# Attention with a top-2 expert layer: constant rows written in place, a looped section for general masks, and expert rows gathered by a row map

## The reference

```python
def _L0_xattn_ref(query, key, value, mask, Wq, bq, Wk, bk, Wv, bv, Wo, bo):
    q = _split_heads(query @ Wq.T + bq)
    k = _split_heads(key @ Wk.T + bk)
    v = _split_heads(value @ Wv.T + bv)
    scores = jnp.einsum('bhqd,bhkd->bhqk', q, k) / jnp.sqrt(jnp.float32(HD))
    scores = jnp.where(mask[:, None, :, :], jnp.finfo(scores.dtype).min, scores)
    attn = jax.nn.softmax(scores, axis=-1)
    ctx = jnp.einsum('bhqk,bhkd->bhqd', attn, v)
    merged = ctx.transpose(0, 2, 1, 3).reshape(query.shape[0], -1, D)
    return merged @ Wo.T + bo

def _L0_ffn_ref(x, gate_w, w1, b1, w2, b2):
    probs = jax.nn.softmax(jnp.einsum('bsd,ed->bse', x, gate_w), axis=-1)
    topk_probs, topk_idx = jax.lax.top_k(probs, TOP_K)
    oh = jax.nn.one_hot(topk_idx, NUM_EXPERTS, dtype=x.dtype)
    h = jnp.einsum('bsd,fed,bske->bskf', x, w1, oh)
    h = jax.nn.gelu(h + jnp.take(b1, topk_idx, axis=0))
    y = jnp.einsum('bskf,def,bske->bskd', h, w2, oh)
    y = y + jnp.take(b2, topk_idx, axis=0)
    return jnp.sum(y * topk_probs[..., None], axis=-2)

x = x + _L0_xattn_ref(_layernorm(x), ctx, ctx, mask, ...)
x = x + _L0_ffn_ref(_layernorm(x), ...)
```

## Time and profile before

| | |
|---|---|
| median of 3 runs | 335.9 us (335.01, 335.9, 337.93) |
| profiled execution | 335.63 us; span 333.9 us; mean granted TensorE clock 0.916 |
| PE busy | 260.5 us (78%) |
| ACT busy | 230.8 us (69%) |
| DVE busy | 170.1 us (51%) |
| POOL busy | 84.7 us (25%) |

### The profile page before, as it was taken

One profiled execution on the slowest core, in us unless ns is written; L12 is line 12 of the kernel. 1 busy time (PEld: TensorE's weight loads), 2 busy tenths in 40 slices (PEclk: granted clock), 3 DMA queues, 4 the chain that ended last, 5 costly groups with the idle time before them and its releaser, 6 DMA issues.

```text
span 333.9 us, 6252 instructions
## 1 busy us (share of the span) xinstructions
PE 260.5 (78%) x1855; PEld 130.2 (39%) x1856; DVE 170.1 (51%) x420; ACT 230.8 (69%) x364; POOL 84.7 (25%) x138
## 2 busy tenths in 40 slices
PE   2587866499999999989899999986484169999940
PEld 2464535122222221212222222235473169999940
DVE  4638966044544535353545454438751047676622
ACT  4366564389999999999999999961794024555520
POOL 8899002100000000000000000402057504444430
PEclk9999895599999999999999999997789559999995
DMA  6999790001101010101001010199201170111115
GB/s 195 381 273 399 291 206 17 5 23 23 34 5 39 0 39 12 28 12 28 18 22 26 14 32 7 39 377 276 36 33 48 48 183 26 32 33 34 31 32 187
DMA packets 29091, 29.57 MB, mean 89 GB/s; under 512 B 15357, under 2 KB 22929, under 8 KB 28944
## 3 DMA queue, kind: packets, MB, share of 16 engines
q1 hardware_dynamic: 27456, 26.21, 26.1%
q0 software_dynamic: 1616, 3.13, 3.2%
HBM read 21.62 MB, written 7.45 MB: 87 GB/s over the span
## 4 chain that ended last, share of the span: by engine, by line
issue 27%; PE 26%; ACT 20%; DVE 7%; DMA 7%; another core or an unknown queue 4%; POOL 3%; SPq 2%; ACTq 1%; DVEq 1%; POOLq 1%
ACT w2T L995 9%; ACT arenaB L995 9%; PE bank L1278 6%; DMA mask_u<-in_mask_BxSxS_bk_dram 5%; PE bank L1397 5%; PE bank L1260 5%; PE bank L1405 3%; DVE arenaB L900 2%; PE bank L1345 2%; PE bank L1169 1%; DMA arenaA<-ys_dram 1%; DVE arenaB L906 1%; PE bank L1355 1%; DVEq L895 1%
## 5 line engine op out<-in xcount | busy, mean ns | idle before, releaser
L717 DVE TENSOR_TENSOR arenaA<-bank,arenaA 128x512 f32<-128x512 f32 x80 | 55.2, 690 | 76.4 <-PE bank L1278 76.4
L995 ACT ACTIVATE arenaB<-bank 128x1024 f32<-128x1024 f32 x80 | 77.5, 1021 | 8.3 <-PE bank L1260 6.2
L995 ACT ACTIVATE w2T<-bank 128x1024 f32<-128x1024 f32 x80 | 76.7, 1030 | 1.3
L1260 PE MATMUL bank<-qS,keys 64*128 64x512 bf16 x324 | 63.2, 389 | 10.1 <-ACT w2T L995 5.7
L1025 ACT ACTIVATE mask_u<-bank,arenaB 128x128 f32<-128x128 f32 x92 | 26.2, 368 | 39.7 <-PE bank L1397 39.7
L1260 PEld LDWEIGHTS bank<-qS,keys 64*128 64x128 bf16 x324 | 15.4, 93 | 97.1 <-ACT w2T L995 49.4
L1278 PE MATMUL bank<-arenaB,vcur 128*32 128x512 f32 x320 | 42.6, 605 | 1.0
L1278 PE MATMUL bank<-w2T,vcur 128*32 128x512 f32 x320 | 42.6, 605 | 0.0
L411 POOL CAST keep<-flags 128x1 f32 x11 | 2.1, 187 | 141.0 <-DVE arenaC L628 140.3
L478 POOL DMA_INDIRECT ys_dram<-arenaB,mask_u x23 | 22.2, 964 | 36.3 <-DVE arenaB L906 36.3
L1397 PE MATMUL bank<-arenaB 128*128 128x128 f32 x184 | 27.4, 296 | 2.8 <-DVE arenaB L892 2.5
(11 more groups left out here) (301 smaller groups left out, 325.7 us busy)
## 6 DMA issues: line engine op xcount, KB each, us to landing
mask_u<-in_L_ffn_w_dram SPq DMA_DIRECT2D x2, 2048.0 KB, 10.6
mask_u<-in_mask_BxSxS_bk_dram SPq DMA_DIRECT2D x6, 560.5 KB, 16.0
ctx_sb<-in_ctx_dram SPq DMA_DIRECT2D x3, 768.0 KB, 13.2
qS<-qparts_dram SPq DMA_DIRECT2D x4, 448.0 KB
mask_u<-in_mask_BxSxS_bk_dram SPq DMA_DIRECT2D x6, 240.0 KB, 11.6
keys_in<-kparts_dram SPq DMA_DIRECT2D x40, 32.0 KB
mask_u<-in_mask_BxSxS_bk_dram SPq DMA_DIRECT2D x1, 1121.0 KB, 8.4
xs_dram<-w1T SPq DMA_DIRECT2D x2, 520.0 KB, 16.8
```

Source lines behind the costliest of these rows:

```text
L717: nc.vector.tensor_tensor(a, bank[:, 4 + k % 2, :], a, ALU.add).then_inc(s["ac"], 1)
L995: nc.scalar.activation(probs[u % 8], bank[:, 2 * (u % 2):2 * (u % 2) + 2, :].rearrange("p a b -> p (a b)"), ACT.Exp, scale=SCALE).then_inc ...
L1260: last = mm(bank[:, 2 * (u % 2) + a, :], keys[rows, g, :], qS[rows, g, cols], start=not hides, stop=True, tile_position=(64 * a, 0))
```

## The change

Ten edits, in the order of the program. Line numbers of the changed kernel are given as "new line".

In the preamble: the constant rows of `qS` come from two memsets on GpSimd instead of a memset and two DMAs. The table `pick` and the third part of the queries are computed on VectorE, between its OR steps, which stand in another order. The first mask tile `mbf` is made on ScalarE. On TensorE the section for `general` masks is a loop over the eight query tiles, with `qcur` copied by GpSimd, instead of written out 16 times; its branch comes after one plan number, and the other two are loaded ahead of the branch on `partial`. The fill of `xs_dram` is gone.

In the second half: rows are no longer scattered with their gates. ScalarE writes all of `xn2` ahead of its weight copies, and SP writes it to `xn_dram` in plain order. VectorE builds 0/1 matrices from the slots, 16 products on TensorE between the two sets of weight transposes turn them into a row map (for each slot the row it holds), and eleven small steps on VectorE, each waiting for the one before, make the row to read and the row to write. GpSimd gathers tiles by indirect DMA, four ahead (`AHEAD`), and in the loop alternates scatter(j) and gather(j+4). Results go to `ys_dram` without gates; the gates come in at the end, with 16 steps of 128 x 128 in place of two adds. The transposes of the gates and the `b2` products moved into the expert loop.

```diff
@@ SP
-            sp.wait_ge(s["scat"], 16 * 2 * QT)
-            for k, (j0, j1) in enumerate(XS_CUTS):
-                sp.dma_start(xs_sb[:, j0:j1, :], xs_dram.rearrange("(j s) c -> s j c", s=P)[:, j0:j1, :]).then_inc(xs_in[k], 16)
+            sp.wait_ge(s["cq_sb"], 2 + QT)
+            sp.dma_start(xn_dram.rearrange("(p t) d -> p t d", t=QT), xn2).then_inc(s["xn_out"], 16)
...
@@ GpSimd, preamble
-            nc.gpsimd.memset(ones_rows, BF16_ONES).then_inc(s["ones_in"], 1)
-            pool.wait_ge(s["ones_in"], 1)
             for w in range(2):
-                pool.dma_start(qS[64 * w:64 * w + 8, :, :].bitcast(F32),
-                               ones_rows.rearrange("p (a q) -> p a q", a=1).broadcast_to([8, G, 512])).then_inc(s["qzero"], 16)
+                nc.gpsimd.memset(qS[64 * w:64 * w + 8, :, :].bitcast(F32), BF16_ONES).then_inc(s["qzero"], 1)
...
-            nc.gpsimd.tensor_scalar(pick, rowkey, iota_p[:, :], None, ALU.is_equal).then_inc(s["pick"], 1)
             pool.wait_ge(s["q_sb"], 2)
             nc.gpsimd.tensor_copy(qparts[:, 1, :], qres).then_inc(s["q_sb"], 1)
-            nc.gpsimd.tensor_tensor(qparts[:, 2, :], qres, qparts[:, 1, :], ALU.subtract).then_inc(s["q_sb"], 1)
...
-            nc.gpsimd.tensor_copy(mbf[:, :, :], mask_u8[:, :, bass.ds(first * P, P)]).then_inc(s["mb"], 1)
...
@@ GpSimd, expert loop
+            def gather(j):
+                nc.gpsimd.indirect_dma_start(xs_sb[:, j, :], None, xn_dram,
+                                             bass.IndirectOffsetOnAxis(ap=x_row[:, j:j + 1].bitcast(U32), axis=0)).then_inc(xs_in[j % AHEAD], 16)
+            pool.wait_ge(s["xn_out"], 16)
+            pool.wait_ge(s["map_sb"], 11)
+            for j in range(AHEAD):
+                gather(j)
             for j in range(NT):
-                pool.wait_ge(s["yacc"], j + 2)
-                nc.gpsimd.indirect_dma_start(ys_dram, bass.IndirectOffsetOnAxis(ap=xs_sb[:, j, ROW - 1:ROW].bitcast(U32), axis=0),
+                pool.wait_ge(s["yacc"], j + 1)
+                nc.gpsimd.indirect_dma_start(ys_dram, bass.IndirectOffsetOnAxis(ap=y_row[:, j:j + 1].bitcast(U32), axis=0),
                                              ysb[:, j % 3, :], None).then_inc(y_out[j % 3], 16)
+                if j + AHEAD < NT:
+                    pool.wait_ge(xs_in[j % AHEAD], 16 * (j // AHEAD + 1))
+                    gather(j + AHEAD)
@@ VectorE, preamble
-            ors(0, 1, 5)
+            ors(0, 1, 2)
+            dve.wait_ge(s["rowkey"], len(COMBOS) + 4)
+            nc.vector.tensor_scalar(pick, rowkey, iota_p[:, :], None, ALU.is_equal).then_inc(s["pick"], 1)
+            ors(0, 2, 4)
...
-            ors(0, 5, QT)
+            ors(0, 4, 6)
+            dve.wait_ge(s["q_sb"], 3)
+            nc.vector.tensor_tensor(qparts[:, 2, :], qres, qparts[:, 1, :], ALU.subtract).then_inc(s["q_sb"], 1)
+            ors(0, 6, QT)
@@ VectorE, behind the slots
+            map_step(nc.vector.tensor_scalar(tile_i, slots, 7, None, ALU.logical_shift_right), 1)
+            map_step(nc.vector.tensor_copy(tile_f, tile_i), 2)
+            map_step(nc.vector.scalar_tensor_tensor(within, tile_f, -float(P), slots_f, ALU.mult, ALU.add), 3)
+            nc.vector.tensor_tensor(in_tile[:, 0:QT, :], cc(within, P)[:, 0:QT, :], iota_q.rearrange("p (a q) -> p a q", a=1).broadcast_to([P, QT, P]), ALU.is_equal)
+            map_step(nc.vector.tensor_tensor(hot_tile, cc(tile_f, NT), ...), 4)
+            nc.vector.tensor_scalar(by_tile[:, :, 0, :], hot_tile, pcol, None, ALU.mult)
+            nc.vector.tensor_tensor(by_tile[:, :, 1, :], hot_tile, cc(ccol, NT), ALU.mult).then_inc(s["map_in"], 1)
+            nc.vector.tensor_tensor(in_tile[:, QT:2 * QT, :], ...).then_inc(s["map_in"], 1)
...
+            dve.wait_ge(s["map_ps"], 1)
+            row_step(nc.vector.tensor_copy(row_f[:, 0:2, 0:NT], bank[:, 2, 0:2 * NT].rearrange("p (a j) -> p a j", a=2)), 1)
+            row_step(nc.vector.tensor_scalar(row_f[:, 2, 0:NT], column, QT - 0.5, None, ALU.is_gt), 2)
...
+            row_step(nc.vector.tensor_copy(y_row, column), 11)
...
-                nc.vector.tensor_scalar(ysb[:, j % 3, :], bank[:, 4 + j % 2, 0:P], xs_sb[:, j, D:D + 1], None, ALU.mult).then_inc(s["yacc"], 1)
+                nc.vector.tensor_copy(ysb[:, j % 3, :], bank[:, 4 + j % 2, 0:P]).then_inc(s["yacc"], 1)
...
-                nc.vector.tensor_tensor(x2, x2, back[k].rearrange("p (t d) -> p t d", d=D), ALU.add).then_inc(s["fin"], 1)
+                for t in range(QT):
+                    nc.vector.scalar_tensor_tensor(x2[:, t, :], back[k][:, t * D:(t + 1) * D], gates[:, k, t:t + 1], x2[:, t, :], ALU.mult, ALU.add).then_inc(s["fin"], 1)
@@ TensorE
-            n = pe.value_load(plan[0:1, 64:65], min_val=1, max_val=T)
             general = pe.value_load(plan[0:1, 65:66], min_val=0, max_val=1)
-            partial = pe.value_load(plan[0:1, 66:67], min_val=0, max_val=T)
             with pe.If(general):
...
+            n = pe.value_load(plan[0:1, 64:65], min_val=1, max_val=T)
+            partial = pe.value_load(plan[0:1, 66:67], min_val=0, max_val=T)
             with pe.If(partial):
...
             expert_weights(0, E)
+            for c in range(2 * QT):
+                last = mm(bank[:, 2, 0:2 * NT], in_tile[:, c, :], by_tile[:, c, :, :].rearrange("p a j -> p (a j)"), start=(c == 0), stop=(c == 2 * QT - 1))
+            last.then_inc(s["map_ps"], 1)
             expert_weights(E, 2 * E)
...
             def slots_turn(j):
-                if j in first:
-                    pe.wait_ge(xs_in[first[j]], 16)
+                pe.wait_ge(xs_in[j % AHEAD], 16 * (j // AHEAD + 1))
```

More of the change, by code:

```diff
@@ L207, in build @@
         oh_b = after[:, 1752:1784].bitcast(BF16)
+        iota_q = after[:, 5888:6016]
+        iota_j = after[:, 6016:6016 + NT]
+        pcol = after[:, 6040:6041]
+        ccol = after[:, 6048:6064]
+        spare = after[:, 6064:6064 + NT]
+        tile_i = after[:, 6088:6104].bitcast(I32)
+        tile_f = after[:, 6104:6120]
+        within = after[:, 6120:6136]
+        row_f = after[:, 6136:6136 + 4 * 24].rearrange("p (a j) -> p a j", a=4)
+        x_row = after[:, 6232:6232 + NT].bitcast(I32)
+        y_row = after[:, 6256:6256 + NT].bitcast(I32)
+        gates = after[:, 6280:6296].rearrange("p (k t) -> p k t", k=2)
         maskw = mask_u8[:, :, :].bitcast(I32)
@@ L878, in _, with row_step @@
             nc.vector.tensor_scalar(tile_e_i, tile_e, float(E - 1), None, ALU.min).then_inc(s["tile_tab"], 1)
[L879 to L884 removed]
+            def row_step(ins, k):
+                ins.then_inc(s["map_sb"], 1)
+                dve.wait_ge(s["map_sb"], k)
@@ new lines, in _ @@
+            row_step(nc.vector.tensor_tensor(column, column, part, ALU.add), 9)
+            row_step(nc.vector.tensor_scalar(column, column, -float(QT), None, ALU.add), 10)
+            row_step(nc.vector.tensor_copy(y_row, column), 11)
+            dve.wait_ge(s["gtexp"], QT + 2)
+            nc.vector.tensor_reduce(g1[:, 2, :], soft[:, :, 0:E], axis=AX.X, op=ALU.add).then_inc(s["gt"], 1)
+            dve.wait_ge(s["gt"], GATE_STEPS + 1)
+            nc.vector.reciprocal(gates[:, 0, :], g1[:, 2, :]).then_inc(s["gt"], 1)
@@ L915, in _ @@
                     slot_rows(j + 2)
-                gated(j)
+                result(j)
+                if j == 2:
+                    for k in range(2):
+                        dve.wait_ge(s["gT_ps"], k + 1)
+                        nc.vector.tensor_copy(epi_e[:, 512 * k:512 * k + 512], bank[0:E, 6 + k, :]).then_inc(s["gT_sb"], 1)
+                if j == 5:
+                    dve.wait_ge(s["b2ps"], 1)
+                    nc.vector.tensor_tensor(x2, x2, bank[:, 6:8, :].rearrange("p a (t d) -> p (a t) d", d=D), ALU.add).then_inc(s["b2ps"], 1)
+            dve.wait_ge(s["b2ps"], 2)
             for k in range(2):
@@ L977, in _ @@
             nc.scalar.activation(arenaA[:, :].rearrange("p (a b) -> p a b", b=512), ones[:, :].rearrange("p (a b) -> p a b", a=1).broadcast_to([P, 8, 512]), ACT.Copy, scale=0.0).then_inc(s["ac"], 1)
+            act.wait_ge(s["plan_ready"], 1)
+            first = act.value_load(plan[0:1, 0:1], min_val=0, max_val=T - 1)
+            nc.scalar.activation(mbf[:, :, :], mask_u8[:, :, bass.ds(first * P, P)], ACT.Copy).then_inc(s["mb"], 1)
             act.wait_ge(s["bd"], 7)
@@ L1005, in _ @@
             nc.scalar.activation(ln[:, 1, :], ln[:, 0, :], ACT.Sqrt).then_inc(s["gtexp"], 1)
+            act.wait_ge(s["sqrt2"], 7)
+            for t in range(QT):
+                nc.scalar.activation(xn2[:, t, :], x2[:, t, :], ACT.Identity, scale=ln[:, 3, t:t + 1], bias=ln[:, 4, t:t + 1]).then_inc(s["cq_sb"], 1)
             nc.scalar.preload_act_table(ACT.Exp)
@@ L1008, in _ @@
             nc.scalar.activation(soft, soft, ACT.Exp).then_inc(s["gtexp"], 1)
-            act.wait_ge(s["xs_fill"], 48)
             for k in range(16):
-                if k == 6:
-                    act.wait_ge(s["sqrt2"], 7)
-                if k in (6, 11):
```

(2 more changed lines are left out.)

177 lines of the change are left out of this document (89 added, 88 removed).

## The result

The changed kernel takes 346.28 us (median of 4 runs, 345.17 to 346.88) against 335.78 for the kernel before: a ratio of 1.027, with a 95% interval of 1.022 to 1.032. It is slower by 10.5 us, where 334.4 was forecast in a range of 327.5 to 342. The profiled execution has a span of 345.2 us, 11.3 more than before. The medians in this document are of all executions of a kernel, while its ratios leave out executions more than 1.5% above its fastest (two of four for after_b, one of four for spread, three of ten for ahead7_pad).

A forecast was written before the change was run, and what follows sets the result against it. The prediction took TensorE to bound the old expert loop, with the attention loop's 156 of 334 us unchanged. Its terms, -3.9 - 13.3 + 13.2 + 2.1 + 0.5 = -1.4, gave 334.4 us, range 327.5 to 342.

The forecast's parts named there:

- the term of the expert loop: First to last result write: 59.3 us against 46.1, so +13.2 us (+7.6 to +17.6).
- The ring: Expert loop: scatter, gather, transposes, down and result copy close over two tiles, 5.6 us or 2.80 a tile, above TensorE's 2.09.
- in part they hit the ring: Expert loop: gates' transposes and `b2` products lie in TensorE's new gaps, partly in the ring: +0.5 us (0 to +1.5).
- rival C: Expert loop: gathers land late, 3.02 a tile, and TensorE, partly idle, loses its clock: 345 us, chance 0.22.
- Rival F: Expert loop: VectorE's staging copies hold back GpSimd's indirect DMAs, up to 0.42 a tile: 342.8 us, chance 0.06.
- The branch: Preamble, TensorE: stall at the branch on `general` goes, -3.9 us; moved loads cost +1.3, the second branch +1.0.
- Rival D: Preamble, TensorE: the branch stall only moves to the second branch, +2.3, giving 336.7 us; chance 0.10.
- The rest of the preamble: Preamble: subtraction leaving GpSimd frees the OR steps, -1.5 us (0 to -1.9); the context tile's copy, -0.8.
- the memsets: Preamble, GpSimd: memsets for `qS` cost nothing, as GpSimd lost other work and the products reading `qS` come 10 us later.
- From the slots to the first product: Stretch from slots ready to the first expert product: -13.3 us (-10.9 to -14.0).
- the end: Behind the last result write: 16 steps of 128 x 128 at 0.29 instead of two adds of 1.24, +2.1 us.
- Rival B: Expert loop: gathers land earlier, only GpSimd's pace of 2.52 a tile holds: 328.8 us, chance 0.15.

The follow-up runs named there:

- after_b: The changed kernel, unedited, run again on another chip: 344.68 us, ratio 1.015 to the kernel before.
- spread: Changed kernel, but empty slots of a tile gather different rows instead of row 0: 342.91 us, ratio 1.015 to the kernel before.
- ahead7_pad: Changed kernel with seven gathers ahead and 26 instructions added to the never-run section for general masks: 335.75 us; on another chip 324.80, then 324.66.
- ahead5_b: Changed kernel with five gathers ahead instead of four, second timing, on another chip: 331.85 us, ratio 0.984 to the kernel before.
- ahead7: Changed kernel with seven gathers ahead instead of four: 327.75 us, ratio 0.973 to the kernel before; 329.25 when run again.
- b2end: Changed kernel with the gates' transposes and `b2` products moved behind the last down: 342.51 us, ratio 1.016 to the kernel before.
- pad13: Kernel of pre_only with 13 transposes (26 instructions) added inside the never-run section for general masks: 328.75 us (one run).
- pre_only: Kernel before with the preamble edits alone, its expert part as before: 333.69 us, ratio 0.989 to the kernel before.

## Why the prediction was wrong

**The step that failed** is the term of the expert loop: "The ring binds 20 of 22 steps: 20 x 2.80 + 3.3 = 59.3". The ring is there, and ahead5_b and ahead7 show that it alone makes the change a loss; its undisturbed length was 5.7 us (forecast 5.6). But I priced the ring as if all its steps always took their least time. The loop came to 71.3, 12.0 more.

The rows of the 19 rings in this trace say where. They took 130.7 us in sum, where 19 times 5.6 is 106.4; two rings run side by side, so this is 12.2 us of the loop. About 10 of it lie in one step, from the start of a gather to the transposes that wait for it: the forecast had 2.4 for it (0.96, 1.3 to 1.4 and 0.1), it took 3.44 on average and never under 2.56. Nine of the gathers took 2.6 to 3.1 (1.4 us of the loop above the forecast). Eight, of tiles with empty slots, took 3.3 to 4.4 (5 us); the forecast knew nothing of these. Those of tiles 7 and 8 took 5.7 and 6.1 (3.5 us), because TensorE was at the b2 products and then, at the lower clock, at what stood behind them, until 276.6 and 280.1; the forecast had 0.5 "in part they hit the ring". The down products at the lower clock add some 1 us. These shares are read from one trace. No run shows them one by one: the loops of b2end and spread are 4.3 and 2.7 shorter, but after_b's is 3.7 shorter with nothing edited and the clock at 0.97.

That rival C's price of 345 came out near the result is luck. Its first half (late gathers in every tile) did not hold, since gathers without empty slots landed 2.5 us after their start, near the forecast's 2.3; and the clock was 0.90 over the loop, where half of the loop at the lower level would be 0.75.

**The range** reached to 342 with 0.28 for slower. Rivals C and F were each priced as one cause alone; in fact several additions to one ring came together, all on one side. That should have put the upper end at C's 345 or beyond.

**The branch** was right in its first half and wrong in its second. The first stall went (3.68 to 0.22). Rival D, the stall at the second branch, had 0.10 and a price of +2.3 over the forecast; it came true (0.42 to 3.70), so that the pair took 3.9 us after the change and 4.1 before. The Trainium skill ("Runtime: NRT & Kernel Launch", section "Instruction fetch mechanics") says a taken branch outside the fetched window waits for a fetch, and pad13 agrees as far as it goes: 26 instructions that never run decide 3.05 us (3369 ns in pre_only, 319 in pad13). The jump's length does not, since the second branch jumps over equally much in all of these kernels. "The nearest row is its own 0.42" was therefore no evidence: the row belonged to another place in the code.

**The rest of the preamble** gave more than forecast: the plan is ready 2.9 us earlier (48.72 to 45.80) against 1.5. That the stretch to the slots came near its forecast (-3.2 against -3.9) is therefore partly luck: 2.3 lost at the branch, 1.4 won here. The OR steps now take 1.4 each, but they also wait less. The forecast took the mask rows to "arrive anyway"; their last landed at 31.6 us before and at 28.9 after. Before, the two DMAs that filled `qS` took 8.8 us to land among them, and the stretch of 20 to 25 us moved 188 GB/s with the DMA engines busy all the time; without them it moves 399, and VectorE, which waited 5.0 us there for a mask row, works:

```profile
qS<-arenaB POOLq DMA_DIRECT2D x2, 128.0 KB, 8.8
```

```profile
20.00:25.00 5.00, 4.09 (x27) 2.35 (x26) 0.42 (x1) 3.74 (x10) 5.00 (x1) 1.00 1.05 188
```

```profile
20.00:25.00 5.00, 4.09 (x24) 2.36 (x24) 4.90 (x5) 3.19 (x8) 4.89 (x3) 1.00 1.04 399
```

No run takes out these DMAs alone. The forecast had the memsets at nothing. They took 8.57 us for the two; GpSimd's copy of the second query part stands behind them, and VectorE waited 0.9 us for it:

```profile
15.28 8.57 POOL L388 MEMSET qS<- 8x4096 f32 x2
```

```profile
27.98 1.23 DVE L574 TENSOR_TENSOR arenaA<-arenaA 128x1024 bf16<-128x1024 f32 x1 [0.93 <-POOL arenaA L398]
```

The table `pick` took 5.1 us on VectorE, not under 3.6, and hid in what had been waits for mask rows.

**From the slots to the first product** -12.9 against -13.3, and **the end** +1.8 against +2.1, were right, and so were their steps: first copy on ScalarE at 242.3, map products at 246.2, first gather at 250.0, each some 3 us earlier in the span than worked out, as everything had moved by 3.2.

Rival B fell (a pace of 2.52 a tile was reached in none of the 19 rings, but ahead7 reached 2.35 once the ring was open). Rival F fell: gathers took 972 ns and writes 988 at the median against 957 before, so some 0.03 for each write can have been lost to VectorE's copies, not 0.42 for a tile. The Trainium skill ("SBUF — State Buffer", section "Who interferes with whom") says that such copies can hold up GpSimd's descriptor writing. The longest issue of the loop took 1242 ns here and 1357 in ahead7, both beside VectorE's copies: 0.3 to 0.4 over the median now and then, and no more.

## What to carry to other kernels

A prefetch distance is set by the ring it closes, not by the count of buffers: write down which instruction the load stands behind on its queue, and divide the whole ring by the tiles it spans; if that is near the engine's pace, one tile more ahead is worth more than any other edit (four ahead 67.6, five 55.9, seven 51.9 us for the same loop on one chip). Price such a ring by the mean of its steps and not by their least, and price what is added inside it on the slow side. Time an unedited kernel twice before you give a few microseconds to an edit of it. And before a stall at a branch is counted as removed, look at where the same stall can go, because the code's place decides it and never-run instructions can move it.
